# Filler work of four engines reordered inside an eleven-step LSTM pipeline: a graph network block on one NeuronCore

## What is computed

```
L0  msg_in  = (adj @ x + bias_in)  * sigmoid(x @ w_in  + b_in)      # same for out; loop = x * sigmoid(x @ w_loop)
    relu(msg_in + msg_out + loop)
L1  A_hat = normalised(adj + I);  h = relu(batchnorm(A_hat @ x @ W1.T + b1));  batchnorm(h @ W2.T + b2)
L2  Wh = x @ W;  e = leaky_relu(s1[:, None] + s2[None, :]), masked by adj;  softmax(e) @ Wh
L3  h = relu(adj @ (x @ Wg0 + bg0));  h = relu(adj @ (h @ Wg1 + bg1))
    for p in 1..4: an LSTM with its own weights over windows of p nodes; its last state replaces node p-1 of each window
```

## Time and profile before

| | |
|---|---|
| median of 3 runs | 627.08 us (626.63 to 627.35) |
| the profiled execution | 628.15 us, of which the span of instructions is 626.4 us |
| PE matmul busy | 598.7 us (96%), weight loads 415.0 us (66%) |
| DVE busy | 484.6 us (77%) |
| ACT busy | 410.4 us (66%) |
| GpSimd (POOL) busy | 239.9 us (38%), 296 instructions |
| granted TensorE clock | 0.998 of full speed |
| DMA | 46.21 MB, mean 74 GB/s |

### The profile page before, as it was taken

How to read it: one execution, slowest core, us unless ns; L and a number is a source line. 1 busy time by engine, 2 the same in 40 slices (tenths; PEclk the granted TensorE clock), 3 DMA queues, 4 the chain that set the end, 5 groups by cost and what they waited for, 6 DMA issues and landing times. The chain is left out here.

```text
span 626.4 us, 9346 instructions
## 1 busy us (share of the span) xinstructions
PE 598.7 (96%) x2520; PEld 415.0 (66%) x2520; DVE 484.6 (77%) x1656; ACT 410.4 (66%) x960; POOL 239.9 (38%) x296
## 2 busy tenths in 40 slices
PE   9999999999798999999989998999999999999994
PEld 6756656446685577568647855874785587577894
DVE  4999999877787867888778887877877766746665
ACT  3667767875754865675757577576757846656764
POOL 1464551005147311841590195059019404401404
PEclk9999999999999999999999999999999999999999
DMA  8334000000301022223033223412222130200201
GB/s 341 136 127 169 1 1 1 0 1 35 101 2 35 38 98 101 97 72 103 34 134 102 75 95 101 136 34 102 68 68 101 48 121 2 100 2 1 102 2 67
DMA packets 23620, 46.21 MB, mean 74 GB/s; under 512 B 2960, under 2 KB 15760, under 8 KB 23440
## 3 DMA queue, kind: packets, MB, share of 16 engines
q1 hardware_dynamic: 23568, 45.62, 20.7%
HBM read 28.29 MB, written 17.33 MB: 73 GB/s over the span
## 5 line engine op out<-in xcount | busy, mean ns | idle before, releaser
L1366 ACT ACTIVATE raw<-QQ,BL 128x256 f32<-128x256 f32 (+2 forms) x279 | 149.5, 558 | 103.6 <-PE QQ L963 69.6
L951 PE MATMUL QQ<-HT,WT 128*128 128x256 f32 (+2 forms) x558 | 183.6, 473 | 1.8 <-DVE HT L2127 1.5
L534 POOL TENSOR_TENSOR RSD<-VAR,pw 128x4 f32<-128x4 f32 (+1 forms) x43 | 58.5, 1360 | 277.2 <-DVE VAR L1833 185.7
L951 PEld LDWEIGHTS QQ<-HT,WT 128*128 128x128 f32 x558 | 104.6, 190 | 59.5 <-issue 33.5
L963 PE MATMUL QQ<-HB,WT 128*128 128x256 f32 (+2 forms) x336 | 100.0, 441 | 2.8 <-DVE HB L2127 2.8
L963 PEld LDWEIGHTS QQ<-HB,WT 128*128 128x128 f32 x336 | 62.5, 190 | 33.9 <-issue 11.7
L2099 DVE SCALAR_TENSOR_TENSOR raw<-raw 128x256 f32<-128x256 f32 (+2 forms) x60 | 36.1, 601 | 30.3 <-ACT raw L1366 30.0
L1402 ACT ACTIVATE raw<-raw 128x256 f32<-128x256 f32 (+4 forms) x79 | 37.2, 470 | 18.2 <-DVE raw L2109 10.1
L600 POOL TENSOR_SCALAR X<-four,MEAN,RSD 128x128 f32<-128x128 f32 x64 | 45.0, 715 | 1.5
L907 PE MATMUL PA<-AD,X 128*128 128x256 f32 x128 | 32.1, 388 | 5.4 <-POOL X L600 5.0
L907 PEld LDWEIGHTS PA<-AD,X 128*128 128x128 f32 x128 | 22.9, 190 | 15.1 <-POOL X L600 11.3
(11 more groups left out here) (253 smaller groups left out, 1185.5 us busy)
## 6 DMA issues: line engine op xcount, KB each, us to landing
turn_e<-HB SPq DMA_DIRECT2D x12, 512.0 KB, 2.6
HB<-turn_e SPq DMA_DIRECT2D x48, 128.0 KB, 2.8
four<-in_x SPq DMA_DIRECT2D x8, 512.0 KB, 3.9
raw<-in_xt SPq DMA_DIRECT2D x8, 512.0 KB, 6.8
turn_t<-HB SPq DMA_DIRECT2D x7, 512.0 KB, 3.5
HB<-turn_t SPq DMA_DIRECT2D x28, 128.0 KB, 2.8
out<-four SPq DMA_DIRECT2D x7, 512.0 KB, 2.7
turn_y<-HB SPq DMA_DIRECT2D x6, 512.0 KB, 3.5
```

What stands on the lines that cost most here:

```text
L534: pool.tensor_tensor(RSD[kk][:, ts], VAR[kk][:, ts], pw[:, ts], ALU.pow).then_inc(ln[k]["rstd"], some)
L951: mm = pe.matmul(steps_view(Q[q], k), WT[:, 0, (p - 1) * 4 + q, :], ht_view(par, k), start=True, stop=(s == 0))
L1366: act.activation(TG[q][:, at:n], Q[q][:, at:n], ACT.Tanh, scale=0.5 if q == G else 0.25, bias=BL[:, p - 1, q:q + 1]).then_inc(g_ok, 1)
```

## The change

Only the order of calls changes, on GpSimd, PE, ACT and DVE, in the start of the attention and in all slots; SP's list is as it was. No operation is added or taken out, none has another shape, no buffer and no semaphore is new. The diff has some 800 lines, all of them moved calls; here are the pieces that the prediction speaks of.

GpSimd, slots 3 to 7, and the start:

```diff
                 N = s + 1 < GROUPS
-                scaled(s + 3)
                 scale1(s)
                 rstd(2, 1, s - 1, 1)
                 scale2(s - 1, 1)
                 t_sum(s - 3)
                 y_sum(s + 1) if N else None
                 rstd(1, 0, s + 1) if N else None
+                tail(s - 3, 1 - par)
                 rstd(2, 1, s, 0)
+                scaled(s + 3)
                 scale2(s, 0)
-                tail(s - 3, 1 - par)
...
             y_sum(2)
+            scaled(4)
             rstd(2, 1, 0, 0)
```

PE, slots 3 to 7 (a piece):

```diff
                 a_project_mix(s - 1, (2,))
+                a_project_mix(s - 1, (3,))
                 a_spread0(s - 1, (0, 1), 0)
-                a_project_mix(s - 1, (3,))
...
                 x(4)
+                a_weigh0(s - 1, 1)
+                a_weigh1(s - 1, 0)
                 x(5)
-                a_weigh0(s - 1, 1)
                 h(5)
+                a_weigh1(s - 1, 1)
                 x(6)
-                a_weigh1(s - 1, 0)
-                a_weigh1(s - 1, 1)
                 h(6)
                 a_spread1(s - 1)
                 x(7)
+                x(8)
                 a_mix(s, (0,))
-                x(8)
                 h(8)
+                a_mix(s, (1,))
```

DVE, slots 3 to 7 (a piece):

```diff
                 inner(3)
                 state(3)
                 a_biased0(s - 1, 0)
+                y_blocks(s + 2) if Y else None
+                e_blocks(s, (0,))
+                inner(4)
                 t_stats(s - 3)
-                inner(4)
+                a_biased0(s - 1, 1)
                 state(4)
                 a_max(s, (3,))
-                e_blocks(s, (0,))
-                a_biased0(s - 1, 1)
                 a_dots(s + 1, 1, 0) if N else None
+                inner(5)
                 a_bias(s, 1)
-                inner(5)
-                e_blocks(s, (1,))
                 state(5)
                 a_biased1(s - 1, 0)
+                a_biased1(s - 1, 1)
+                e_blocks(s, (1,))
```

More of the change, by code:

```diff
@@ L688, in _ @@
             scale2(1)
-            scaled(4)
             slots(slot)
@@ L1043, in slot @@
                 if s == LAST + 1:
-                    a_mix(LAST, (3,))
                     x(0)
@@ L1047, in slot @@
                     x(1)
+                    a_spread0(LAST, (0, 1), 0)
+                    a_mix(LAST, (3,))
+                    x(2)
+                    spin(PB[:, BANK:BANK + P], 4)
                     a_project_mix(LAST, (3,))
-                    a_spread0(LAST, (0, 1), 0)
-                    x(2)
                     x(3)
@@ L1068, in slot @@
                     h(9)
-                    spin(PB[:, BANK:BANK + P], 4)
                     x(10)
@@ L1106, in slot @@
                     t_turn_half(par, 0)
+                    spin(Q[F][:, 0:P], 8)
                     t_turn_half(par, 1)
-                    spin(Q[F][:, 0:P], 8)
                     return
@@ L1167, in _ @@
             a_turn_e(0, (1,))
+            a_attend(0, (0,))
+            a_attend(0, (1,))
+            a_project(1, 1)
+            a_turn_e(0, (2,))
             a_scores(1, 1)
-            a_attend(0, (0,))
-            a_project(1, 1)
-            a_attend(0, (1,))
-            a_turn_e(0, (2,))
             a_turn_e(0, (3,))
@@ L2274, in slot @@
                     state(9)
-                    a_s12(s + 1)
+                    a_sum2_mix(s, (0,))
                     a_sum2_mix(s, (1,))
+                    inner(10)
                     a_stats2(s, 0)
-                    inner(10)
+                    state(10)
                     a_small2(s, 0)
-                    state(10)
                     return
@@ L2284, in slot @@
                     state(0)
+                    a_sum2_mix(s - 1, (2,))
                     inner(1)
                     state(1)
-                    a_sum2_mix(s - 1, (2,))
+                    inner(2)
                     a_sum2_mix(s - 1, (3,))
+                    state(2)
                     a_stats2(s - 1, 1)
                     a_small2(s - 1, 1)
-                    inner(2)
-                    state(2)
                     t_blocks(s - 3)
@@ L2307, in slot @@
                     state(7)
-                    t_stats(s - 3)
                     inner(8)
@@ L2373, in slot @@
                 inner(1)
+                state(1)
                 a_sum2_mix(s - 1, (2,))
-                state(1)
+                a_sum2_mix(s - 1, (3,))
+                t_blocks(s - 3)
+                a_stats2(s - 1, 1)
+                inner(2)
                 a_max(s, (1,))
-                a_sum2_mix(s - 1, (3,))
+                state(2)
                 a_bias(s, 0)
-                t_blocks(s - 3)
-                inner(2)
+                a_small2(s - 1, 1)
                 a_max(s, (2,))
-                state(2)
-                a_stats2(s - 1, 1)
-                a_small2(s - 1, 1)
-                y_blocks(s + 2) if Y else None
                 inner(3)
@@ L2388, in slot @@
                 a_biased0(s - 1, 0)
+                y_blocks(s + 2) if Y else None
+                e_blocks(s, (0,))
+                inner(4)
                 t_stats(s - 3)
-                inner(4)
+                a_biased0(s - 1, 1)
                 state(4)
                 a_max(s, (3,))
-                e_blocks(s, (0,))
-                a_biased0(s - 1, 1)
                 a_dots(s + 1, 1, 0) if N else None
+                inner(5)
                 a_bias(s, 1)
-                inner(5)
-                e_blocks(s, (1,))
                 state(5)
                 a_biased1(s - 1, 0)
+                a_biased1(s - 1, 1)
+                e_blocks(s, (1,))
+                a_dots(s + 1, 0, 0) if N else None
+                inner(6)
+                a_inverse(s)
                 e_blocks(s, (2,))
-                a_biased1(s - 1, 1)
-                inner(6)
+                state(6)
                 a_stats1(s + 1, 0) if N else None
-                state(6)
-                a_stats1(s + 1, 1) if N else None
-                a_dots(s + 1, 0, 0) if N else None
+                a_hidden(s - 1, 1 - par)
+                inner(7)
                 e_blocks(s, (3,))
-                inner(7)
-                a_dots(s + 1, 0, 1) if N else None
                 state(7)
                 a_dots(s + 1, 1, 1) if N else None
-                a_hidden(s - 1, 1 - par)
-                a_inverse(s)
+                a_stats1(s + 1, 1) if N else None
+                a_small1(s + 1) if N else None
                 inner(8)
@@ L2417, in slot @@
                 state(8)
-                a_small1(s + 1) if N else None
+                a_dots(s + 1, 0, 1) if N else None
                 a_sum2_mix(s, (0,))
```

244 lines of the change are left out of this document (122 added, 122 removed).

## The result

The changed kernel takes **619.32 us** (median of 4 runs, 618.56 to 620.16), the kernel before 627.22 in the same comparison. The ratio is 0.9863, 95% interval 0.9850 to 0.9877: 8.6 us or 1.4% faster, far over the 0.2% that a measurement tells. The prediction was 618.7, with a range of 613.5 to 625.8. PE's matmuls now cover 97% of a span of 616.7 us.

The account below looks back on a forecast made before the run. PE was taken as the bound (matmuls cover 96% of the span), its idle time being what counts. 5.5 + 3.0 + 3.4 - 3.5 = 8.4 us less turns 627.08 into 618.7 us, range 613.5 to 625.8.

Parts of the forecast that it names:

- a: Slots 3 to 7: the tail moved into GpSimd's pause ends PE's waits for L600; 5.5 us gained, bounds 3 and 6.2.
- c: Slots 3 to 7: inner(4) ahead of t_stats on DVE ends h(5)'s wait; 3.0 us gained, bounds 1 and 3.8.
- e: Places with 0 to 0.3 us slack: one hidden-state wait of 0.7 us in five slots; 3.5 us lost, bounds 1 and 8.
- d: Start of the attention: first copy of weights ahead of the statistics on DVE; 3.4 us gained, bounds 1 and 4.9.
- b: Output DMA on SP: the LSTM output's turn leaves 1.9 us earlier, so t_sum can start earlier; worth nothing alone.
- Rival 1: DVE's deliveries become PE's wait: another 1 us lost in each of five slots, 5 us go back, 623.7 us; 22%.
- Rival 2: The tail beside steps 9 and 10 holds strand operations on DVE, 4 us a slot, 635 us; 8%.
- Rival 3: PE's waits for L600 return as waits for the hidden state, start gains under 1 us; 626 to 628 us; 7%.
- The rule weighed in the prediction: Moved pows and tail would cost the strand around h(9) up to 1.6 us a slot, the sum some 8 us smaller.

Follow-up runs that it names:

- e4_tail_back: The changed kernel with GpSimd's list of slots 3 to 7 as in the kernel before: 620.56 us, ratio 0.9874.
- e7_tstats_first: The changed kernel with t_stats ahead of inner(4) on DVE again in slots 3 to 7: 619.39 us, ratio 0.9865.
- e3_tail_alone: The kernel before with only GpSimd's list of slots 3 to 7 new (tail and scaled moved): 625.79 us, ratio 0.9965.
- e12_tsum_halved: The changed kernel with each t_sum operation of 512 columns on GpSimd issued as two of 256: 618.11 us, ratio 0.9833.
- e5_hold_tsum: The changed kernel with one more GpSimd wait, holding t_sum until the hidden state of step 3 is written: 614.73 us, ratio 0.9789.

## Why the prediction was right, and where its steps were not

The forecast of 8.4 us less met 8.6 by the ratio and 7.9 by the medians. The sum is nearly exact, and that is in part luck. Slots 3 to 7 (terms a, c and e) gave 6.0 us where the terms make 5.0, the start 4.1 where d says 3.4, and slots 2, 8 and 9, priced at nothing, lost about 2: these errors nearly cancel. Of the terms, one held with its cause, three had a good size with a wrong cause or place, and one was missing.

**a) The tail fills the pause (5.5 us).** The wait went, all of it. The step that failed is "the tail's place does it": its place alone gave 2.2 us, and taken back it cost 0.7, within the uncertainty. The earlier `a_small2(s, 0)` on DVE, which the step named in half a sentence, frees the same queue, and with the tail back in its old place it is worth 5.5. The reading under it was right: GpSimd's queue was full from 359.92 on (it ran to 384.2, the end of `y_sum`, and not to 381.8).

**b) The output DMA** left early as said: L503 at 350.66 and L469 at 361.12. `t_sum` now starts 1.75 us behind L917 (369.74 - 367.99), where it was 3.36 in the kernel before, but the DMA is not the reason. In e4_tail_back the output DMA is late again (L503 at 361.21, L469 at 363.00), and `t_sum` still starts 1.82 us behind L917 (371.52 - 369.70), right behind L600, as it did in the kernel before: what makes it early is that L600 is early. I priced an earlier `t_sum` at nothing. It was not nothing: it is what meets the hidden state of step 3.

**c) `inner(4)` ahead of `t_stats` (3.0 us).** The wait of `h(5)` went. The cause given first, `t_stats`' place, was wrong (e7_tstats_first: no change). What is left are the early `t_sum` and PE's filler ahead of `x(5)`, and they were not taken apart in one experiment. The early `t_sum` can do it alone: in e3_tail_alone, with PE's and DVE's old lists, the wait is gone in the two slots where `t_sum` starts 1.88 us behind L917, although there `x(4)` starts later too, by its own wait. Whether PE's filler was needed as well is not shown. That `inner(4)` is not stretched in slot 5 is luck of the meeting point with `y_sum`; it starts 1.25 us after `y_sum` there, and in e12_tsum_halved, where it starts 0.42 us after it, it took 1.22 us again.

**d) The start (3.4 us)** is confirmed with its cause: 4.1 us for the start alone, 4.5 us lost when the one call goes back (of which about 1 us is the clock, which the kernel before did not lose). The term was 0.7 us too small, within the uncertainty of the measurement. The profile names what it left out: slot 2 begins 3.5 us earlier (189.80 against 193.34), as forecast, and the 1.53 us that L951 waited in slot 2, which the prediction set aside with the waits that are single or lie where the order stays, fall to 0.50.

**e) Given back (3.5 us).** The size is right, 0.71 us in each of five slots, 3.6 in all by the rows of the changed kernel and e5_hold_tsum (2.65 - 1.94), and the place wrong. I named `h(3)`, `h(5)`, `a_mix(s, 0)` and `h(9)` as places of little slack. None waits; `x(4)` does, which was not on my list, for an operation that GpSimd held. The nearest row, a wait for the hidden state of 0.5 to 0.7 us, gave the size by kind, not by mechanism.

**Missing: slot 9.** I left slots 2, 8 and 9 at nothing, plus or minus 1 us. Their new lists lose 2.4 us, 1.8 of it by the profiles in slot 9. This is why 4.1 and 6.0 do not add up to the whole.

**The rivals.** Rival 1 (weights late for L889): one wait of 0.4 us, in slot 2, not the 1 us a slot. Rival 2 (the tail blocks the strand): the tail runs beside step 9, and the holds are there but small. The changed kernel, cell operations of 256 columns on DVE beside the tail at the end of slots 4 and 5, and one beside `scaled` (L592):

```profile
344.99 0.55 DVE L2099 SCALAR_TENSOR_TENSOR raw<-raw 128x256 f32<-128x256 f32 x1 [0.37 <-ACT raw L1366]
...
399.43 0.42 DVE L2105 SCALAR_TENSOR_TENSOR raw<-raw 128x256 f32<-128x256 f32 x1 [0.17 <-ACT raw L1366]
```

```profile
351.05 1.20 POOL L592 TENSOR_SCALAR HB<-HB,BN 128x1024 f32<-128x1024 f32 x1
...
351.70 0.82 DVE L2127 SCALAR_TENSOR_TENSOR HT<-raw 128x256 f32<-128x256 f32 x1 [0.55 <-ACT raw L1402]
```

Beside the tail such an operation takes 0.42 to 0.55 us in slots 3 to 7, so it loses some 0.12 us at most, where the rival charged 0.5. Its mechanism was real with longer instructions: `t_sum`'s, and `scaled`'s, whose hold (0.82 us) fell where PE waited for nothing. Rival 3 fell with the waits.

**The rule weighed in the prediction.** The Trainium skill (page "SBUF — State Buffer", section "Who interferes with whom") lets a DVE operation with two SBUF inputs and a GpSimd operation that reads SBUF exclude each other for a whole operation. By these rows that is what happens between DVE's cell operations and GpSimd's `tensor_tensor` of 256 and 512 columns: the DVE operation ends 0.28 us after the GpSimd operation that it met (the changed kernel and e12_tsum_halved). It is what happens with `tensor_scalar` too: L2127 at 351.70 ends at 352.51, 0.27 us after the 1024 columns of L592. One of 128 columns takes 0.45 us when it meets nobody (L613 at 344.39), so that it can hold little, and where DVE's operation was first, GpSimd's is the one that grows: L613 took 0.61 us at 345.25. The one form that does not follow the rule is `pow`: the cell operation at 408.21 ran its 0.42 us in the middle of it, and L2105 at 350.19 in the changed kernel its 0.42. So the row at 408.21 was evidence for `pow` alone. I took its price, nothing, for all of GpSimd's operations, and should have asked of each how long it is.

## What to carry to other kernels

Before moving filler, list which pairs of operations on the two engines stretch each other, with the length of each, and check that no long one meets the strand at its new time; a filler that is made early is not free. Where it does meet, a semaphore wait that holds the filler for the strand's operation can be worth half a reordering: here one line gave 4.6 us, and all the moved calls 8.6. Undo single calls after a large reordering: of this one, the lists of slots 2, 8 and 9 lost 2.4 us, one call in the start was worth half of the gain, and two lists (PE's and DVE's) only make sense together.
